# The last convolution's rows by way of scratch memory and a ring of four buffers

## The chip, the cores and the metric

One core of a Trainium2 chip runs the kernel. The metric is the time of one execution on the device, in microseconds (us), as the median of three runs. A profiled execution gives the trace from which all rows below are read.

## What is computed

The input x is 4 images of 64 channels and 128 x 128 pixels, float32. Four blocks follow one another, each with a residual and each on a group norm of what came before:

```python
x = x + L0(gn(x))   # super tokens and attention
x = x + L1(gn(x))   # grouped convolution, weights routed per image
x = x + L2(gn(x))   # depthwise convolutions, deformable sampling, selective scan
x = x + L3(gn(x))   # this change

def L3(x, w3, w1, b, p=4):
    m3 = (j - i) % p == 0                     # which input channels go through 3x3
    out = conv3x3(x, w3 * m3, padding=1)
    out = out + einsum('oi,bihw->bohw', w1 * ~m3, x)
    return out + b.sum(axis=1)
```

Only the last line of the four, the convolution L3 with its group norm, and the sampling and scan at the end of L2 concern this case.

## The kernel before

Images are worked in pairs: 2 images x 64 channels fill the 128 partitions, and `Fori(0, PAIRS)` runs the whole network twice, once per pair. Everything of a pair lies in `X` (128 x 128 rows x 128). Each engine has its own program written out in order; they meet through semaphores, and a wait on an engine holds all that stands behind it on that engine. All DMAs are issued by SP, on one queue.

The sampling and scan (`sample_and_scan_*`, lines 730 to 1005) walk over 32 chunks of four rows. DVE line 781 adds the block's result to a chunk of `X` and raises `sc_x`; the value `pair * NT + c + 1 + CREDIT` says that chunk c is final. The sampling reads its image from `PAD`, which shares its memory (`BIG`) with `RAW3`, so `RAW3` can be written only after the sampling.

The last convolution works with output rows in pairs and with one image at a time: `RAW3[half, q, j]` holds, for image q, the odd rows of X on partitions 0 to 63 and the even rows on 64 to 127, so that two output rows come from one matmul. `pair_rows(n)` (lines 501 to 512, SP) fills it in eight parts of 1 MB, two DMAs each (lines 508 and 511), from the moment at which all 32 chunks are final; part n waits until part n-2 has landed. Then SP waits for the last two parts (line 516) and begins its loop over the 16 strips of eight row pairs (NS = 16): wait for `cv_done` of strip S, two output DMAs (line 526), and, while another pair follows, the load of one strip of the next pair's input (line 456).

For a strip S the work goes: ACT `normed_rows(S)` (lines 1830 to 1844) norms its rows in place in `RAW3` and raises `l3_xn`; POOL (651, 652) and DVE (641, 642) make the four column sums; PE `columns_pe` (line 667, 16 matmuls) waits for `cv_done` of strip S-2, whose PSUM banks it takes; ACT `add_columns_act` (line 686) moves two of the four sums to `OBUF`, after the output DMA of strip S-2; DVE (692 to 697) adds the rest and raises `cv_done`. ACT's order is written out by hand:

```python
for S in range(3):
    normed_rows(S)
for S in range(NS):
    if S + 3 < NS:
        normed_rows(S + 3)
    add_columns_act(act, pair, S)
```

So on ACT the norm of strip S+3 stands ahead of the add of strip S.

Of the kernel before, what the change touches and what calls it, by code (L numbers as in the profile page):

```python
# [82 lines left out]
WTAIL = UNITS * UPIX - PROWS * PW  # L83
BACK = (UNITS // 2 + 2) * 16
PARTS3 = 8
SPREAD = [(WINDOWS + 1 - k) // 2 * 16 for k in range(2)]
MOVES = [n + PARTS3 * 16 for n in SPREAD]
EXPT = EXPERTS * 8 * 36
NRT = EXPT + FC + 2 * P

# [17 lines left out]
def program(nc, x, vec, mat, dts, rows, fc, sel, far_sel, cst, out):  # L108
    ctx = ExitStack()
    with ctx:  # L110
# [34 lines left out]
        IDB = sb("IDB", [P, P], BF16)  # L145
        RI = sb("RI", [P, 1], I32)
        spill, back_spill = (nc.dram_tensor(n, (WINDOWS, P, WROW * W), F32).ap() for n in ("spill", "back_spill"))
        rt_spill = nc.dram_tensor("rt_spill", (P, NRT), F32).ap()
        SMG = sb("SMG", [P, 160])
        UNIT, ROW16, CHAN8, HALF2, ROWPART = (sb(n, [P, w]) for n, w in  # L150
# [142 lines left out]
        r = Region()  # L293
        r.at = cols_end
        OBUF = r.take(2, 2 * CH)


        load = sem("load")
# [28 lines left out]
        l1_val, l1_tv, l1_tp, l1_mm, from_psum, l1_res, l1_st = steps(  # L327
            "l1_val", "l1_tv", "l1_tp", "l1_mm", "from_psum", "l1_res", "l1_st")
        moved, l1_back = [sem(f"moved{k}") for k in range(2)], sem("l1_back")
        l1_out = [sem(f"l1_out{k}") for k in range(RING)]  # L330
        cv_vector, cv_pool, cv_mm, cv_part, cv_done = (sem(n) for n in (
            "cv_vector", "cv_pool", "cv_mm", "cv_part", "cv_done"))
        rt_pe, rt_dve, rt_act = sem("rt_pe"), sem("rt_dve"), sem("rt_act")
# [67 lines left out]

        def parts_moved(pair, n):

            return pair * MOVES[n % 2] + SPREAD[n % 2] + (n // 2 + 1) * 32

        def strip_done(pair, c):

# [33 lines left out]
        @block.sync  # L441
        def _(sp):

            for lo in (0, C):
                sp.dma_start(VECS[lo:lo + C, :], vec).then_inc(load, 16)
                sp.dma_start(MATS[lo:lo + C, :], mat).then_inc(load, 16)
            sp.dma_start(DTS[:, :], dts).then_inc(load, 16)
            sp.dma_start(ROWV[:, :], rows).then_inc(load, 16)
            sp.dma_start(CSTS[:, :], cst).then_inc(load, 16)
            sp.dma_start(SELF, sel.rearrange("r t c -> r (t c)")).then_inc(load, 16)  # L450
            sp.dma_start(FSEL[:, :, :], far_sel).then_inc(load, 16)
            for k in range(2):
                sp.sem_inc(out_dma[k], 32)

            def load_strip(c, first_row):
                sp.dma_start(X[:, c * 8:c * 8 + 8, :], x[bass.ds(first_row, P), c * 8:c * 8 + 8, :]).then_inc(x_in[c // 4], 16)

            for c in range(NS):
                load_strip(c, 0)
            sp.wait_ge(const_act, 3)  # L460
            sp.dma_start(rt_spill, RT).then_inc(rt_saved, 16)
            with sp.Fori(0, PAIRS) as pair:

                def spread(w):

                    sp.wait_ge(moved[w % 2], pair * MOVES[w % 2] + (w // 2 + 1) * 16)
                    settle(sp)
                    sp.dma_start(WN[:, :, w * W:(w + 1) * W],
                                 spill[w].rearrange("(u c) (r x) -> (c r) u x", u=UNITS, x=W)).then_inc(l1_in, 16)

                for w in range(WINDOWS):
                    sp.wait_ge(o_x, pair * NS + (window_strip(w) + 1 + CREDIT))
                    if w == WINDOWS - 1:
                        sp.wait_ge(l1_sq, (pair + 1) * (2 * NS) + CREDIT)
                        for j in range(4):
                            sp.dma_start(FCT[:, 4 * j:4 * j + 4], fc[:, 4 * j:4 * j + 4]).then_inc(fc_in[j // 2], 16)
                    sp.dma_start(spill[w], X[:, STEP * w:STEP * w + WROW, :].rearrange("p r x -> p (r x)")).then_inc(moved[w % 2], 16)
                    if w >= 1:
                        spread(w - 1)
                spread(WINDOWS - 1)  # L480
                sp.dma_start(RT, rt_spill).then_inc(rt_in, 16)

                def back(u):

                    for v in (u, u + 1):
                        sp.wait_ge(l1_out[v % RING], pair * (UNITS // RING * 16) + (v // RING + 1) * 16)
                    sp.dma_start(X[u * WCH:(u + 2) * WCH, 1:H - 1, :].rearrange("c (v r) x -> c v (r x)", v=WINDOWS),
                                 back_spill[:, u * WCH:(u + 2) * WCH, W:(WROW - 1) * W].rearrange(
                                     "v c n -> c v n")).then_inc(l1_back, 16)

                for u in range(UNITS):
                    sp.wait_ge(l1_res, pair * UNITS + (u + 1))
                    sp.dma_start(back_spill[:, u * WCH:(u + 1) * WCH, :].rearrange("v c (r x) -> (c r) v x", x=W),
                                 OB1[:, u % RING, :].rearrange("p (v x) -> p v x", x=W)).then_inc(l1_out[u % RING], 16)
                    if u % 2 == 1 and u >= 3:
                        back(u - 3)
                back(UNITS - 2)
                for w, r, row in ((0, 0, 0), (WINDOWS - 1, WROW - 1, H - 1)):
                    sp.dma_start(X[:, row, :], back_spill[w, :, r * W:(r + 1) * W]).then_inc(l1_back, 16)

                def pair_rows(n):

                    if n >= 2:
                        sp.wait_ge(moved[n % 2], parts_moved(pair, n - 2))
                        settle(sp)
                    q, i = n // 4, n % 4
                    a = 16 * i + 1
                    sp.dma_start(RAW3[0:C, q, a:a + 16, 1:1 + W],
                                 X[q * C:(q + 1) * C, 2 * a - 1:2 * a + 30:2, :]).then_inc(moved[n % 2], 16)
                    lo, hi = (0 if i == 0 else a), min(a + 16, H // 2)  # L510
                    sp.dma_start(RAW3[C:P, q, lo:hi, 1:1 + W],
                                 X[q * C:(q + 1) * C, 2 * lo:2 * hi - 1:2, :]).then_inc(moved[n % 2], 16)

                sp.wait_ge(sc_x, (pair + 1) * NT + CREDIT)
                settle(sp)
                for n in range(PARTS3):
                    pair_rows(n)
                for n in (PARTS3 - 2, PARTS3 - 1):
                    sp.wait_ge(moved[n % 2], parts_moved(pair, n))
                    settle(sp)  # L520
                for S in range(NS):
                    q, t, k = S // 8, S % 8, S % 2
                    sp.wait_ge(cv_done, pair * NS + (S + 1 + CREDIT))
                    settle(sp)
                    for h in range(2):
                        sp.dma_start(out[bass.ds(pair * P + q * C, C), 16 * t + h:16 * t + 15 + h:2, :],
                                     OBUF[h * C:(h + 1) * C, k, :].rearrange("p (r w) -> p r w", r=8)).then_inc(out_dma[k], 16)
                    with sp.If(pair < PAIRS - 1):
                        load_strip(S, nc.s_assert_within(pair * P + P, 0, (PAIRS - 1) * P,
                                                         skip_runtime_bounds_check_because="the branch was taken"))  # L530
            for k in range(2):
                sp.wait_ge(out_dma[k], 32 * (PAIRS * NS // 2 + 1))
# [1023 lines left out]
        def _(pool):  # L1556
            credit(pool, cv_pool, df_w9, df_r1, df_lo, df_add, sc_u)
            pool.memset(PAD[:, :, :], 0.0).then_inc(border, 1)
            with pool.Fori(0, PAIRS) as pair:

                pool.wait_ge(border, pair * 3 + 1)
                pool.wait_ge(const_dve, 10)
                pool.wait_ge(rt_saved, 16)
                pool.wait_ge(cv_done, pair * NS + CREDIT)
                for k in range(2):
                    pool.wait_ge(out_dma[k], pair * (NS * 16) + 32)
# [50 lines left out]
        def _(act):  # L1617
# [18 lines left out]
                               banks(0, 3)[:, k * n:(k + 1) * n].rearrange("p (t k o) -> p k t o", t=9, k=8), ACT.Copy)  # L1636
            act.activation(FCB, PSUM[:, 3, 0:FC], ACT.Copy)
            act.activation(TO_CHANNEL, PSUM[:, 3, FC:FC + P], ACT.Copy).then_inc(const_act, 1)
            act.wait_ge(rt_saved, 16)
            settle(act)  # L1640

            def group_norm(n):
# [6 lines left out]
            with act.Fori(0, PAIRS) as pair:  # L1649
# [106 lines left out]
                def evacuate(u):  # L1756
# [2 lines left out]
                        act.wait_ge(l1_val, (pair + 1) * 16)  # L1759
                    if u >= RING:  # L1760
                        act.wait_ge(l1_st, pair * (2 * UNITS) + (2 * (u - RING) + 1))
                        act.wait_ge(l1_out[u % RING], pair * (UNITS // RING * 16) + (u // RING) * 16)
                    act.activation(OB1[:, u % RING, :].rearrange("p (a n) -> p a n", a=3),
                                   PSUM[:, 3 * (u % 2):3 * (u % 2) + 3, 0:3 * W], ACT.Identity,
                                   bias=SMW[:, 3, u:u + 1]).then_inc(from_psum, 1)
# [64 lines left out]
                def normed_rows(S):  # L1830

                    q, t = S // 8, S % 8
                    act.wait_ge(moved[S // 2 % 2], parts_moved(pair, S // 2))
                    settle(act)

                    def rows(lo, hi, j0, j1):
                        a = RAW3[lo:hi, q, j0:j1, 1:1 + W]
                        return act.activation(a, a, ACT.Identity, bias=NORM3[lo:hi, q, 0:1], scale=NORM3[lo:hi, q, 1:2])

                    if t == 0:  # L1840
                        rows(C, P, 0, 1)
                    if t == 7:
                        rows(0, C, ODD - 1, ODD)
                    rows(0, P, 8 * t + 1, min(8 * t + 9, ODD - 1)).then_inc(l3_xn, 1)
# [386 lines left out]
```

## Time and profile before

| | |
|---|---|
| median of three runs | 2919.49 us (2916.44 to 2926.07) |
| profiled execution, its own time | 2928.06 us |
| its span | 2926.2 us |
| PE busy | 2370.3 us, 81% of the span |
| DVE busy | 2004.0 us, 68% |
| ACT busy | 1412.5 us, 48% |
| POOL busy | 1119.8 us, 38% |
| DMA, mean over the span | 47 GB/s |
| BIG<-X, 512 KB each | 24 DMAs, median 8.6 us to landing |
| X<-x, 512 KB each | 32 DMAs, 7.5 us |
| out<-BIG, 256 KB each | 64 DMAs, 3.6 us |

The span holds two passes of the same work, one per pair; the last convolution of the first pair lies between about 1329 and 1477 us, that of the second between 2774 and 2926. A busy share over the whole span says little about a stage of 150 us; the rows for the change are those of these two stretches and of the sampling before them.

### The profile page before, as it was taken

To read this page: it belongs to the slowest core of one execution; us is meant where nothing else is said; L and a number is where in the kernel's file an instruction comes from. 1 tells how busy PE (TensorE), PEld (TensorE's weight loads), DVE (VectorE), ACT (ScalarE), POOL (GpSimd) and SP (SyncE) were. 2 spreads that over 40 slices of the span, in tenths; PEclk is the share of its full clock that TensorE was granted. 3 is DMA by queue.
4 is the path that set the end of the run, shared out by engine and by line. 5 is a ranking of instruction groups with operands and counts; after the bars stand their busy time and mean duration, and the time that the engine had idled before them with its cause. 6 is when DMAs were issued, how large, how long until landed. Compare 5 with 4: busy or idle time off the path is not lost.

```text
span 2926.2 us, 32644 instructions
## 1 busy us (share of the span) xinstructions
PE 2370.3 (81%) x8311; PEld 1249.8 (43%) x8311; DVE 2004.0 (68%) x3313; ACT 1412.5 (48%) x2140; POOL 1119.8 (38%) x967
## 2 busy tenths in 40 slices
PE   3897769599978888885968967786899688888778
PEld 2595535244433333332426954352344333333233
DVE  5544656398858999984555447464988589999844
ACT  2632433385754555552345336235677455555422
POOL 2200019280017777762311000374600377777422
PEclk9898889799979999997978989897999799999979
DMA  4000269500000000008610005492000000000083
GB/s 156 1 1 1 98 231 162 81 0 1 1 0 1 0 0 0 0 1 148 155 44 1 1 0 196 163 182 32 1 0 1 0 1 0 0 0 0 12 140 79
DMA packets 126795, 138.18 MB, mean 47 GB/s; under 512 B 3895, under 2 KB 106943, under 8 KB 123351
## 3 DMA queue, kind: packets, MB, share of 16 engines
q1 hardware_dynamic: 126679, 136.82, 20.3%
q8 instruction: 49, 0.80, 0.1%
q14 instruction: 67, 0.55, 0.1%
HBM read 64.65 MB, written 55.38 MB: 41 GB/s over the span
## 4 chain that ended last, share of the span: by engine, by line
PE 54%; DVE 18%; issue 10%; DMA 7%; ACT 5%; POOL 3%; DVEq 2%; SPq 1%; ACTq 0%; POOLq 0%
PE PSUM L1891 9%; PE PSUM L2069 7%; PE PSUM L667 6%; PE PSUM L959 4%; POOL BIG L868 3%; DMA BIG<-X 3%; DVE BIG L794 3%; PE PSUM L1934 2%; DVE BIG L770 2%; PE PSUM L2127 2%; PE PSUM L2121 2%; PE PSUM L2083 2%; PE PSUM L1948 2%; PE PSUM L953 2%; PE PSUM L1951 2%
## 5 line engine op out<-in xcount | busy, mean ns | idle before, releaser
L770 DVE TENSOR_TENSOR BIG<-PSUM,BIG 128x512 f32<-128x512 f32 x576 | 383.5, 684 | 100.7 <-POOL BIG L868 30.3
L1019 DVE SCALAR_TENSOR_TENSOR PSUM<-BIG,VECS,PSUM 128x1024 f32<-128x1024 f32 x272 | 350.3, 1288 | 119.7 <-PE PSUM L1891 113.4
L868 POOL TENSOR_TENSOR BIG<-BIG 128x512 f32<-128x512 f32 x256 | 346.0, 1351 | 147.5 <-DVE BIG L817 129.5
L708 POOL TENSOR_TENSOR BIG<-TOEP,BIG 128x384 f32<-128x384 f32 x84 | 97.1, 1182 | 611.6 <-DVE BIG L1417 611.6
L1891 PE MATMUL PSUM<-BIG,WDW 128*128 128x512 f32 x704 | 317.4, 601 | 9.0 <-ACT BIG L1802 9.0
L953 PE MATMUL PSUM<-BIG,SELB 120*128 120x512 bf16 x576 | 224.5, 392 | 120.1 <-DVE BIG L770 116.0
L959 PE MATMUL PSUM<-BIG,CSTS 128*128 128x512 f32 x512 | 270.5, 610 | 0.0
L849 POOL TENSOR_TENSOR BIG<-BIG 128x96 f32<-128x96 f32 x192 | 68.8, 384 | 382.3 <-ACT BIG L910 382.3
L1891 PEld LDWEIGHTS PSUM<-BIG,WDW 128*128 128x128 f32 x704 | 132.4, 191 | 168.4 <-issue 157.3
L953 PEld LDWEIGHTS PSUM<-BIG,SELB 120*128 120x128 bf16 x576 | 56.0, 97 | 345.7 <-DVE BIG L770 297.8
L2069 PE MATMUL PSUM<-BIG 128*128 128x381 f32 (+1 forms) x576 | 190.6, 495 | 15.2 <-DVE BIG L715 15.2
L667 PE MATMUL PSUM<-BIG,WL 128*128 128x512 f32 x256 | 126.0, 639 | 42.2 <-DVE BIG L697 26.0
L2069 PEld LDWEIGHTS PSUM<-BIG 128*128 128x128 f32 x576 | 112.0, 195 | 93.2 <-issue 20.6
L959 PEld LDWEIGHTS PSUM<-BIG,CSTS 128*128 128x128 f32 x512 | 101.8, 199 | 73.7 <-issue 63.9
L686 ACT ACTIVATE BIG<-PSUM,SM 128x512 f32<-128x512 f32 x64 | 42.5, 721 | 183.0 <-PE PSUM L667 140.6
L1595 POOL TENSOR_TENSOR BIG<-BIG 128x1024 f32<-128x1024 f32 x32 | 75.6, 2363 | 117.9 <-ACT BIG L1790 117.9
L692 DVE TENSOR_TENSOR BIG<-BIG,PSUM 128x512 f32<-128x512 f32 x32 | 22.4, 698 | 140.8 <-ACT BIG L686 140.8
L856 POOL TENSOR_TENSOR BIG<-BIG 128x320 f32<-128x320 f32 x64 | 98.8, 1544 | 42.7 <-ACT BIG L899 42.7
L667 PE MATMUL PSUM<-BIG,WMID 128*128 128x512 f32 x256 | 115.1, 592 | 0.0
L876 POOL TENSOR_TENSOR BIG<-BIG 128x512 f32<-128x512 f32 x64 | 108.7, 1699 | 13.5 <-DVE BIG L826 13.5
L651 POOL TENSOR_TENSOR BIG<-BIG 128x576 f32<-128x576 f32 x32 | 37.9, 1184 | 186.4 <-issue 110.3
L894 ACT ACTIVATE BIG<-PSUM 128x512 f32<-128x512 f32 x64 | 38.2, 597 | 145.6 <-DVE X L781 141.9
(347 smaller groups left out, 5276.9 us busy)
## 6 DMA issues: line engine op xcount, KB each, us to landing
spill<-X SPq DMA_DIRECT2D x18, 1024.0 KB, 6.4
back_spill<-BIG SPq DMA_DIRECT2D x32, 576.0 KB, 7.8
X<-x SPq DMA_DIRECT2D x32, 512.0 KB, 7.5
out<-BIG SPq DMA_DIRECT2D x64, 256.0 KB, 3.6
X<-back_spill SPq DMA_DIRECT2D x16, 1008.0 KB, 15.4
BIG<-X SPq DMA_DIRECT2D x24, 512.0 KB, 8.6
BIG<-fc SPq DMA_DIRECT2D x8, 1024.0 KB, 9.6
BIG<-X SPq DMA_DIRECT2D x4, 544.0 KB, 9.1
```

Source lines behind the costliest of these rows:

```text
L667: ins = pe.matmul(PSUM[:, 4 * k + m, :].rearrange("p (r j) -> p r j", r=8), w, VC[:, k, m, b:b + 8, :], start=(b == 0), stop=(b == 1))
L708: eng.tensor_tensor(to.rearrange("p (x c r) -> p x c r", x=3, r=WROW), TOEP[:, y].unsqueeze(1).unsqueeze(1).broadcast_to([P, 3, WCH, WROW] ...
L770: dve.tensor_tensor(img(o), img(PSUM[:, (k + q) % 2, :]), pch(c, XBASE, dy, dx), ALU.mult).then_inc(df_p, 1)
L794: dve.tensor_tensor_scan(HH[:, k, :], DA, UU, SM[:, 12:13] if first else HH[:, 1 - k, CH - 1:CH], ALU.mult, ALU.add).then_inc(sc_h, 1)
L856: pool.tensor_tensor(w9h, w9h, part(0), ALU.subtract).then_inc(df_r1, 1)
L868: pool.tensor_tensor(XS[:, k, :], XS[:, k, :], PRD[:, product_buffer(q), :], ALU.add).then_inc(df_add, 1)
L876: pool.tensor_tensor(UU, RL, XS[:, (k + 1) % 2, :], ALU.mult).then_inc(sc_u, 1)
L953: pe.matmul(PSUM[:, (k + q) % 2, :], SELB[:, q, :], WTB[0:WROWS, k, h * CH:(h + 1) * CH], start=True, stop=True).then_inc(df_w, 1)
L959: pe.matmul(PSUM[:, ACC, :], ident, PRD[:, m % 2, :], start=(m == 0), stop=(m == PE_SUMS - 1)).then_inc(df_acc, 1)
L1019: return dve.scalar_tensor_tensor(out=rows8(to), in0=strip(c, base, dy, dx), scalar=vc(weights, j), in1=rows8(acc), op0=ALU.mult, op1=ALU.add)
L1891: ins = pe.matmul(img(acc[:, h * CH:(h + 1) * CH]), w[:, j - stored, :], strip(c, base, dy, dx)[:, h * ROWS:(h + 1) * ROWS, :], start=(j = ...
L2069: ins = pe.matmul(to, WIDE[:, u % RING, x, :], v, start=(x == 1), stop=(x == 2))
```

## The change

The rows for the convolution no longer go from `X` to `RAW3` directly. `pair_rows(n)` now waits only until the chunks of its 16 rows of X are final, and writes them, split into odd and even rows, to a scratch tensor in device memory, `rows_spill`: four DMAs of 256 KB for each of the eight parts, the first seven of them while the sampling runs. A new `stage(S)` reads a strip's rows from there, 4 KB or 4.5 KB on each partition, into one of four buffers (`STAGE`), which lie in memory that the sampling used. Stages 0 to 3 are issued behind `pair_rows(7)`; stage S+4 is issued in SP's loop, after the wait for `cv_done` of strip S and the two output DMAs of S. `normed_rows(S)` waits for its stage instead of for the part, and writes from `STAGE` to `RAW3` instead of in place. The border rows of `rows_spill` are zeroed once at the start by four small DMAs, for which ACT and POOL wait together with the saving of the routing tables. The semaphores `l1_out` become `slot_dma` and count further, with no other effect on the block L1.

```diff
+STAGES = 4
-MOVES = [n + PARTS3 * 16 for n in SPREAD]
+MOVES = [n + PARTS3 * 32 for n in SPREAD]
...
+        rows_spill = nc.dram_tensor("rows_spill", (2, 2, C, ODD, W), F32).ap()
...
+        STAGE = r.take(STAGES, 9 * W)
...
             sp.dma_start(rt_spill, RT).then_inc(rt_saved, 16)
+            for q in range(2):
+                sp.dma_start(rows_spill[q, 0, :, 0, :], cs("zero")[0:C, 0:W]).then_inc(rt_saved, 16)
+                sp.dma_start(rows_spill[q, 1, :, ODD - 1, :], cs("zero")[C:P, 0:W]).then_inc(rt_saved, 16)
...
                 def pair_rows(n):
 
+                    sp.wait_ge(sc_x, pair * NT + (4 * n + 4 + CREDIT))
+                    settle(sp)
                     if n >= 2:
                         sp.wait_ge(moved[n % 2], parts_moved(pair, n - 2))
                         settle(sp)
-                    q, i = n // 4, n % 4
-                    a = 16 * i + 1
-                    sp.dma_start(RAW3[0:C, q, a:a + 16, 1:1 + W],
-                                 X[q * C:(q + 1) * C, 2 * a - 1:2 * a + 30:2, :]).then_inc(moved[n % 2], 16)
-                    lo, hi = (0 if i == 0 else a), min(a + 16, H // 2)
-                    sp.dma_start(RAW3[C:P, q, lo:hi, 1:1 + W],
-                                 X[q * C:(q + 1) * C, 2 * lo:2 * hi - 1:2, :]).then_inc(moved[n % 2], 16)
-
-                sp.wait_ge(sc_x, (pair + 1) * NT + CREDIT)
-                settle(sp)
+                    for q in range(2):
+                        sp.dma_start(rows_spill[q, 0, :, 8 * n + 1:8 * n + 9, :],
+                                     X[q * C:(q + 1) * C, 16 * n + 1:16 * n + 16:2, :]).then_inc(moved[n % 2], 16)
+                        sp.dma_start(rows_spill[q, 1, :, 8 * n:8 * n + 8, :],
+                                     X[q * C:(q + 1) * C, 16 * n:16 * n + 15:2, :]).then_inc(moved[n % 2], 16)
+
+                def stage(S):
+
+                    q, t = S // 8, S % 8
+                    if t == 0 or t == 6:
+                        for n in ((5, 6) if t == 0 else (7,)):
+                            sp.wait_ge(moved[n % 2], parts_moved(pair, n))
+                            settle(sp)
+                    if S >= STAGES:
+                        sp.wait_ge(l3_xn, pair * NS + (S - STAGES + 1))
+                        settle(sp)
+                    lo = 0 if t == 0 else 1
+                    sp.dma_start(STAGE[:, S % STAGES, lo * W:9 * W],
+                                 rows_spill[q, :, :, 8 * t + lo:8 * t + 9, :].rearrange("h c j x -> (h c) (j x)")).then_inc(
+                                     slot_dma[S % STAGES], 16)
+
                 for n in range(PARTS3):
                     pair_rows(n)
-                for n in (PARTS3 - 2, PARTS3 - 1):
-                    sp.wait_ge(moved[n % 2], parts_moved(pair, n))
-                    settle(sp)
+                for S in range(STAGES):
+                    stage(S)
                 for S in range(NS):
                     q, t, k = S // 8, S % 8, S % 2
                     sp.wait_ge(cv_done, pair * NS + (S + 1 + CREDIT))
@@
                         sp.dma_start(out[bass.ds(pair * P + q * C, C), 16 * t + h:16 * t + 15 + h:2, :],
                                      OBUF[h * C:(h + 1) * C, k, :].rearrange("p (r w) -> p r w", r=8)).then_inc(out_dma[k], 16)
+                    if S + STAGES < NS:
+                        stage(S + STAGES)
                     with sp.If(pair < PAIRS - 1):
...
-                pool.wait_ge(rt_saved, 16)
+                pool.wait_ge(rt_saved, 80)
...
-            act.wait_ge(rt_saved, 16)
+            act.wait_ge(rt_saved, 80)
...
                 def normed_rows(S):
 
                     q, t = S // 8, S % 8
-                    act.wait_ge(moved[S // 2 % 2], parts_moved(pair, S // 2))
+                    act.wait_ge(slot_dma[S % STAGES], pair * (UNITS // RING * 16 + NS // STAGES * 16)
+                                + (UNITS // RING * 16 + (S // STAGES + 1) * 16))
                     settle(act)
 
                     def rows(lo, hi, j0, j1):
-                        a = RAW3[lo:hi, q, j0:j1, 1:1 + W]
-                        return act.activation(a, a, ACT.Identity, bias=NORM3[lo:hi, q, 0:1], scale=NORM3[lo:hi, q, 1:2])
+                        a = STAGE[lo:hi, S % STAGES, (j0 - 8 * t) * W:(j1 - 8 * t) * W].rearrange("p (j x) -> p j x", x=W)
+                        return act.activation(RAW3[lo:hi, q, j0:j1, 1:1 + W], a, ACT.Identity,
+                                              bias=NORM3[lo:hi, q, 0:1], scale=NORM3[lo:hi, q, 1:2])
```

## Rows read from the trace of the kernel before

**Rows 1.** The page, part 4: the chain that ended last, by engine.

```profile
PE 54%; DVE 18%; issue 10%; DMA 7%; ACT 5%; POOL 3%; DVEq 2%; SPq 1%; ACTq 0%; POOLq 0%
```

**Rows 2.** Waits of SP's queue, 1320 to 1480: total us, times, longest us.

```profile
SPq L354 <- DVE X L781: 794.8, 1, 794.8
...
SPq L354 <- DMA BIG<-X: 19.5, 8, 5.8
```

**Rows 3.** Timeline of SP, first pair: start us, us, what it issues.

```profile
1329.48 0.69 SPq L508 DMA_DIRECT2D BIG<-X  x1
...
1406.79 1.40 SPq L526 DMA_DIRECT2D out<-BIG  x2
1408.33 0.80 SPq L456 DMA_DIRECT2D X<-x  x1
...
1475.41 1.41 SPq L526 DMA_DIRECT2D out<-BIG  x2
```

**Rows 4.** Timeline of ACT, both pairs' last convolutions.

```profile
1337.89 2.88 ACT L1838 ACTIVATE BIG<-BIG,SM 64x128 f32<-64x128 f32 x3 [3.75 <-DMA BIG<-X]
...
1402.70 1.34 ACT L686 ACTIVATE BIG<-PSUM,SM 128x512 f32<-128x512 f32 x2 [3.71 <-PE PSUM L667]
...
2828.72 1.24 ACT L1838 ACTIVATE BIG<-BIG,SM 128x1024 f32<-128x1024 f32 x1
2829.94 1.33 ACT L686 ACTIVATE BIG<-PSUM,SM 128x512 f32<-128x512 f32 x2
```

**Rows 5.** Timeline of PE, both pairs' last convolutions; [idle before <-releaser].

```profile
1343.20 6.75 PE L667 MATMUL PSUM<-BIG,WL 128*128 128x512 f32 x8 [8.09 <-POOL BIG L652]
...
1386.81 5.45 PE L667 MATMUL PSUM<-BIG,WL 128*128 128x512 f32 x8 [12.83 <-DVE BIG L697]
...
1395.53 3.60 PE L667 MATMUL PSUM<-BIG,WL 128*128 128x512 f32 x8
...
1402.39 3.60 PE L667 MATMUL PSUM<-BIG,WL 128*128 128x512 f32 x8
...
2787.87 6.34 PE L667 MATMUL PSUM<-BIG,WL 128*128 128x512 f32 x8 [8.13 <-POOL BIG L652]
...
2797.47 3.60 PE L667 MATMUL PSUM<-BIG,WL 128*128 128x512 f32 x8
```

**Rows 6.** Windows: length, busy per engine, PEclk, DMA share, GB/s; sampling, PE's first strip.

```profile
880.00:1325.00 445.00, 373.08 (x1139) 154.17 (x1137) 391.87 (x559) 239.49 (x455) 326.58 (x302) 0.98 0.00 0
...
1343.00:1350.00 7.00, 6.80 (x9) 0.54 1.25 185
```

**Rows 7.** Landings, issue to landing: lines 456, 526 (1370 to 1490), 508, 511.

```profile
DMA to landing us min/median/max: 4.7/5.2/6.0
DMA to landing us min/median/max: 3.2/3.6/5.0
DMA to landing us min/median/max: 5.0/8.4/9.7
DMA to landing us min/median/max: 7.6/10.6/10.9
```

**Rows 8.** Timeline of DVE, both pairs' last convolutions.

```profile
1356.76 0.69 DVE L697 TENSOR_TENSOR BIG<-BIG,PSUM 128x512 f32<-128x512 f32 x1
...
1404.08 0.70 DVE L692 TENSOR_TENSOR BIG<-BIG,PSUM 128x512 f32<-128x512 f32 x1 [3.01 <-ACT BIG L686]
...
2801.01 0.68 DVE L697 TENSOR_TENSOR BIG<-BIG,PSUM 128x512 f32<-128x512 f32 x1
...
2920.42 0.68 DVE L697 TENSOR_TENSOR BIG<-BIG,PSUM 128x512 f32<-128x512 f32 x1
```

**Rows 9.** Timeline of PE in the block before, four matmuls after a gap.

```profile
834.37 3.47 PE L2121 MATMUL PSUM<-BIG,CSTS 128*128 128x512 f32 x4 [4.04 <-DVE BIG L1019]
```

**Rows 10.** Timeline of ACT at the start of the kernel.

```profile
53.61 1.28 ACT L1650 ACT_TABLE_LOAD   x1 [3.64 <-DMA rt_spill<-BIG]
56.85 0.26 ACT L1644 ACTIVATE SM<-PSUM,GNE 128x1 f32<-128x1 f32 x1 [1.97 <-PE PSUM L1885]
```

More of the change, by code:

```diff
@@ L329, in program @@
         moved, l1_back = [sem(f"moved{k}") for k in range(2)], sem("l1_back")
-        l1_out = [sem(f"l1_out{k}") for k in range(RING)]
+        slot_dma = [sem(f"slot_dma{k}") for k in range(RING)]
         cv_vector, cv_pool, cv_mm, cv_part, cv_done = (sem(n) for n in (
@@ L402, in parts_moved @@
         def parts_moved(pair, n):
-            return pair * MOVES[n % 2] + SPREAD[n % 2] + (n // 2 + 1) * 32
+            return pair * MOVES[n % 2] + SPREAD[n % 2] + (n // 2 + 1) * 64
         def strip_done(pair, c):
@@ L485, in back @@
                     for v in (u, u + 1):
-                        sp.wait_ge(l1_out[v % RING], pair * (UNITS // RING * 16) + (v // RING + 1) * 16)
+                        sp.wait_ge(slot_dma[v % RING], pair * (UNITS // RING * 16 + NS // STAGES * 16) + (v // RING + 1) * 16)
                     sp.dma_start(X[u * WCH:(u + 2) * WCH, 1:H - 1, :].rearrange("c (v r) x -> c v (r x)", v=WINDOWS),
@@ L493, in _ @@
                     sp.dma_start(back_spill[:, u * WCH:(u + 1) * WCH, :].rearrange("v c (r x) -> (c r) v x", x=W),
-                                 OB1[:, u % RING, :].rearrange("p (v x) -> p v x", x=W)).then_inc(l1_out[u % RING], 16)
+                                 OB1[:, u % RING, :].rearrange("p (v x) -> p v x", x=W)).then_inc(slot_dma[u % RING], 16)
                     if u % 2 == 1 and u >= 3:
@@ L1761, in evacuate @@
                         act.wait_ge(l1_st, pair * (2 * UNITS) + (2 * (u - RING) + 1))
-                        act.wait_ge(l1_out[u % RING], pair * (UNITS // RING * 16) + (u // RING) * 16)
+                        act.wait_ge(slot_dma[u % RING], pair * (UNITS // RING * 16 + NS // STAGES * 16) + (u // RING) * 16)
                     act.activation(OB1[:, u % RING, :].rearrange("p (a n) -> p a n", a=3),
```

## The prediction

> **What bounds the kernel now.** The page comes first: the chain of work that ended last is PE for 54%, with DMA at 7% [rows 1]. That is the whole span; the change lives in two stretches of some 150 us and in the samplings before them, so the waits and timelines of those stretches decide. The waits of SP's queue [rows 2] show SP idle for 794.8 us until the last chunk of X is final (DVE line 781) and then held 19.5 us in eight waits by its own moves to RAW3. SP's timeline shows the first move at 1329.48 [rows 3]; ACT gets its first rows at 1337.89, 8.4 us later [rows 4]; PE's first strip starts at 1343.20 after 8.09 us idle, and PE stops once more for 12.83 us before 1386.81 [rows 5]. That second gap has a DVE releaser, but ACT's queue explains it: its add of strip 2 could not write OBUF before the output of strip 0, which SP issues only after all its moves. So the moves cost the head of the stretch and one gap in its middle. From 1395.53 on PE takes a strip of 16 matmuls every 6.86 us (1395.53 to 1402.39) with no gap: there PE is the bound, and DMA, ACT, DVE and POOL keep up.
>
> **The change, part by part.** *Removed*: the seven first parts leave the end of the sampling, and SP's wait for parts 6 and 7 ahead of its strip loop. The 12.83 us gap goes with it.
>
> *Moved into the sampling*: 28 DMAs of 256 KB per pair. In 445 us of sampling the DMA share is 0.00, and SP has nothing else to issue [rows 6, 2]. What it could cost is DVE's reading of X beside them. I take 0; if each DVE instruction became 1% longer it would be 4 us a pair (391.87 us busy), and below zero nothing can come, as no engine gives work away. The end of the sampling stays.
>
> *Head*: behind the last chunk now come part 7 (four DMAs, the same 1 MB as part 0 had) and stage 0 behind it in the same queue. Part 0 landed 8.4 us after its issue; stage 0 adds 4.5 KB x 128 partitions. In pairs of moves the first lands after 8.4 us and the second, issued about 0.7 us later, after 10.6 [rows 7]: 2.9 us apart for half a megabyte each, so one follows the other instead of sharing. An input strip of about that size, issued 1.54 us behind an output of 512 KB, lands in 5.2, so one of these larger pieces takes about 2 us itself. I take 2.15 us later for ACT's first norm and PE's start; bounds 0 (shared engines, both done with part 7) and 4. Stages 1 to 3 follow at about 2 us each, by 1347, before PE ends strip 0 at about 1355: nothing waits for them.
>
> *The ring, which is where the time goes.* Stage S+4 is issued after `cv_done` of S. On ACT its norm, `normed_rows(S+4)`, stands ahead of `add_columns_act(S+1)`. What waits behind ACT's new wait is therefore that add, and with it DVE's adds and `cv_done` of S+1, which releases stage S+5. Four buffers do not open this circle: the wait binds ACT's order, not the data that PE reads next. One turn, from SP's output issue of one strip to that of the next:
> - output issues until the next DMA: 1406.79 to 1408.33 [rows 3], 1.54;
> - landing. The nearest row is the input strip X<-x, which stands in exactly this place behind the same output, comes from device memory, has 512 KB and 4 KB per partition: 5.2 (4.7 to 6.0) [rows 7];
> - ACT wakes: 0.05;
> - the norm until the add behind it starts: 2828.72 to 2829.94 [rows 4], 1.22;
> - add until DVE's first add: 1402.70 to 1404.08 [rows 4, 8], 1.38;
> - DVE's four adds until SP's next issue: 1404.08 to 1406.79 [rows 8, 3], 2.71.
>
> The sum is 12.10 us against PE's 6.86. Stages 4 to 15 each make one turn: 12 turns, 145.2 us per pair. In the second pair no input strip is issued behind the stage; by the order seen above that changes nothing.
>
> *Tail*: after `cv_done` of strip 12 only PE binds. Strip 14 starts about 0.1 us ahead of that strip's output issue, two strips take 13.7, and from the end of PE's strip to SP's issue it is 4.4 (1402.39 to 1406.79) [rows 5, 3]: 18.0. PE now has gaps of about 5 us between strips. After a gap of 4.04 us four matmuls took 3.47 [rows 9], as slow as the first eight of a strip after 8.09 (6.75), in whose window the granted clock was 0.54, so mostly 1.2 GHz [rows 6]; eight at 2.4 GHz take 3.43 (half of the 6.86). Such a strip takes 10.2 us instead of 6.9. That still fits into a turn of 12.1; in the tail it can cost 0 to 3.3, and I take 1.6.
>
> *Start*: four small DMAs behind rt_spill. ACT waited for rt_spill until 53.6, loaded a table for 1.28 and then waited 1.97 us more for PE [rows 10]; that wait covers them. 0, at most 1. The two other new waits on SP (parts 5 to 7, `l3_xn`) are for things long done; what is queued behind them is only the strip loop. The norm keeps its size.
>
> **The sum.** First pair: the first output can be issued at 1357.45 (end of line 697 of strip 0) + 0.22, that is 1357.67 [rows 8]. Then 1357.67 + 2.15 + 145.2 + 18.0 + 1.6 = 1524.6 for the issue of the last output, which was 1475.41 [rows 3]: +49.2. Second pair: 2801.69 + 0.22 + 167.0 = 2968.9, against 2921.1 + 0.22 = 2921.3 [rows 8]: +47.5. Together +96.7 us. The profiled execution took 2928.06, so its like becomes 3024.8. The median of the runs lies 8.6 us below it, and 2919.49 + 96.7 = **3016.2 us**, 3.3% slower.
>
> The Trainium skill ("DMA: Bandwidth & Descriptors", section "Anatomy of one DMA — SWDGE (gpsimd) path") gives a DMA about 2.0 us fixed plus its bytes at 436 GB/s, measured on another issuing path than SP's; for a stage an estimate from it is 3.2 us, and 2968 in all. The traced 5.2 us contradicts it for a transfer behind another, and the sum goes by the trace.
>
> **Rivals.**
> - *Short landing* (0.05): the stage lands as fast as a lone output does, 3.2 us [rows 7], if the output ahead does not delay it. Each of the 24 turns is 2.0 shorter: 2968. Against it: X<-x in the same place never took under 4.7. This is the time that the page's fit gives.
> - *PE takes the turn* (0.05): if PE's clock stayed at 1.2 GHz for all matmuls a strip would take 13.7, more than 12.1, and bind: 24 x 1.6 = +38, 3055. Against: a PE without gaps has been at 2.4 GHz after its first eight matmuls each time.
> - *The landing is later* (0.07): in the first pair the next input strip, issued 0.8 us behind the stage, shares the engines with it. With 8.4 us, as a BIG<-X that had another behind it, 12 turns grow by 3.2: +38, 3055. The 2.9 us distance speaks against.
> - *Faster, because the ring hides the fetch* (0.02): place, ACT's wait for the stage. If that wait never ended last, PE would run on from 1345.35: first strip 10.0, fifteen by 6.86, 4.4, so the last issue at 1462.7 (-12.8); in the second pair from 2790.0 with 9.6 for the first strip [rows 5], 2906.9 (-14.4): 2892. It decides against the forecast only if a turn is under 8.1 us (12.1 - 96.7 / 24), which needs a landing in 1.2. No landing in [rows 7] is near. It could only be right if I read ACT's order wrongly.
> - *The writes do not go beside the sampling* (0.01): if they slowed it or came at its end as before, the gain at the head goes too; seven parts per pair at 5.8 us (twice the 2.9) are +81, 3097.
>
> **How the numbers follow.** The forecast has 0.80. Its own bounds: landings of 4.7 to 6.0 give -12 to +19 over 24 turns, the head -4 to +4, the tail -3 to +3, start and sampling 0 to +9: 2997 to 3051. To leave out no more than 0.2 in all, and as the two rivals at 3055 lie just beyond, the range is 2995 to 3056. A measurement of this kernel can tell about 0.3% (9 us) from no change; every case but the fourth is slower by more: slower 0.97, same 0.01, faster 0.02.
>
> **What the profile after would show.** SP issues at line 526 some 12 us apart for strips 1 to 12 and 7 apart at the end. ACT's norm released by DMA BIG<-rows_spill twelve times per pair, 4 to 6 us each, and its add directly behind the norm. PE idle about 2 or 5 us before each strip. The gap of 12.83 gone, PE's start in the stretch some 2 us later. DMA in the sampling above zero, with DVE's busy time there unchanged. The prediction is wrong if the outputs stay 6.9 us apart, or if the landing of a stage is not near 5.2.

## The result, and the profile after

The changed kernel takes 3022.55 us (median of four runs, 3020.13 to 3023.89) against 2922.78 for the kernel before, run beside it. The ratio is 1.0347, with a 95% interval from 1.0333 to 1.0361: 3.5% slower, about 100 us, where 96.7 and 3016.2 us had been forecast. The profiled executions took 2928.06 and 3023.75 us.

Line numbers of the new kernel are some 20 higher: ACT's norm is line 1859 (was 1838), its add 706 (686), DVE's adds 712 to 717 (692 to 697), PE's matmuls 687 (667), the stage 531, the outputs 544 (526).

The page, parts 1, 4 and 6. DVE, ACT and POOL are busy for the same time as before; PE is busy 30 us longer with the same matmuls, because more of them ran at a lower granted clock (see "PE's clock" below). In the chain DMA has risen from 7% to 8%, and a line that did not exist before stands third in it:

```profile
PE 2400.3 (79%) x8311; PEld 1257.1 (42%) x8311; DVE 2004.2 (66%) x3313; ACT 1412.2 (47%) x2140; POOL 1121.4 (37%) x967
...
PE 48%; DVE 19%; issue 11%; DMA 8%; ACT 6%; POOL 3%; DVEq 2%; SPq 2%; ACTq 0%; POOLq 0%
PE PSUM L1913 9%; PE PSUM L2091 6%; DMA BIG<-rows_spill 4%; PE PSUM L979 4%; POOL BIG L888 3%; DVE BIG L814 3%; PE PSUM L1956 2%; PE PSUM L687 2%; DVE BIG L790 2%; PE PSUM L2149 2%; PE PSUM L1970 2%; PE PSUM L2105 2%; PE PSUM L2143 2%; PE PSUM L973 2%; PE PSUM L2131 2%
...
BIG<-rows_spill SPq DMA_DIRECT2D x28, 512.0 KB, 5.4
```

The same line in part 5 says who waits for it: ACT's norm. In the kernel before it also waited for DMAs, but 13.2 us in all and only at the head of the stretches [rows 4]; now it waits 246.6 us in all:

```profile
L1859 ACT ACTIVATE BIG<-BIG,SM 128x1024 f32<-128x1024 f32 (+2 forms) x40 | 42.7, 1080 | 246.7 <-DMA BIG<-rows_spill 246.6
```

The timeline of SP in the first pair's last convolution, to set beside [rows 3]. The outputs, 6.8 us apart before, are 11.9 to 13.0 apart here for strips 0 to 12; the DMA of a stage is mostly issued 1.5 to 1.7 us behind the first output DMA:

```profile
1329.17 0.57 SPq L515 DMA_DIRECT2D rows_spill<-X  x1
...
1358.11 1.49 SPq L544 DMA_DIRECT2D out<-BIG  x2
...
1395.51 1.42 SPq L544 DMA_DIRECT2D out<-BIG  x2
1397.05 0.81 SPq L531 DMA_DIRECT2D BIG<-rows_spill  x1
...
1408.02 1.42 SPq L544 DMA_DIRECT2D out<-BIG  x2
...
1507.44 1.41 SPq L544 DMA_DIRECT2D out<-BIG  x2
...
1528.07 1.40 SPq L544 DMA_DIRECT2D out<-BIG  x2
```

One turn of the circle, as the chain of work that ended last shows it, each step released by the one above it: the DMA, then the two pieces of a norm, the add, DVE's adds, the outputs, the next DMA. No PE instruction is in it:

```profile
1397.05 5.41 DMA BIG<-rows_spill
1402.50 0.07 issue
1402.57 0.09 ACT BIG L1859
...
1402.97 1.12 ACT BIG L1859
1404.09 1.20 ACT BIG L706 x2
1405.31 0.06 DVE BIG L712
...
1407.11 0.69 DVE BIG L717
...
1408.02 0.62 SPq L544
...
1409.69 5.50 DMA BIG<-rows_spill
```

Twice in the first pair (at 1420.81 and 1481.89) the view goes over a strip of PE's instead of a DMA. The add that follows there belongs to the strip before that one, whose matmuls had ended 11.6 and 14.1 us earlier; PE's end and the norm's end only fall together in time. In the second pair no such step stands between the DMAs.

ACT and PE in the same stretch, beside [rows 4] and [rows 5]. ACT waits 10 us for a stage, norms it, and only then, with no idle time between, adds a strip whose matmuls were long done (PE had ended strip 2 at 1367.5, and its add starts at 1379.12). PE's releaser is DVE's last add: PE waits for PSUM banks that are still held until the late adds of an earlier strip are done.

```profile
1377.97 1.24 ACT L1859 ACTIVATE BIG<-BIG,SM 128x1024 f32<-128x1024 f32 x1 [10.13 <-DMA BIG<-rows_spill]
1379.12 1.29 ACT L706 ACTIVATE BIG<-PSUM,SM 128x512 f32<-128x512 f32 x2
1390.33 1.24 ACT L1859 ACTIVATE BIG<-BIG,SM 128x1024 f32<-128x1024 f32 x1 [9.92 <-DMA BIG<-rows_spill]
```

```profile
1344.66 5.69 PE L687 MATMUL PSUM<-BIG,WL 128*128 128x512 f32 x8 [9.99 <-POOL BIG L672]
...
1370.41 3.70 PE L687 MATMUL PSUM<-BIG,WL 128*128 128x512 f32 x8 [2.89 <-DVE BIG L717]
1373.94 3.60 PE L687 MATMUL PSUM<-BIG,WMID 128*128 128x512 f32 x8
1382.98 5.33 PE L687 MATMUL PSUM<-BIG,WL 128*128 128x512 f32 x8 [5.44 <-DVE BIG L717]
```

The sampling, the window of [rows 6]: DVE's busy time is 391.64 us against 391.87, with a DMA share of 0.07 where it was 0.00.

```profile
880.00:1325.00 445.00, 371.77 (x1139) 153.69 (x1137) 391.64 (x559) 239.97 (x456) 326.81 (x302) 0.98 0.07 17
```

### The profile page after: what moved, and what is told of

Its sections match the earlier page's. It is cut to its first block, busy times and chain, and to the rows that moved or that the text cites. A ratio compares the mean times of both kernels' runs of the same rounds, so it can differ in the third digit from the quotient of the medians.

```text
span 3021.9 us, 32766 instructions
## 1 busy us (share of the span) xinstructions
PE 2400.3 (79%) x8311; PEld 1257.1 (42%) x8311; DVE 2004.2 (66%) x3313; ACT 1412.2 (47%) x2140; POOL 1121.4 (37%) x967
## 4 chain that ended last, share of the span: by engine, by line
PE 48%; DVE 19%; issue 11%; DMA 8%; ACT 6%; POOL 3%; DVEq 2%; SPq 2%; ACTq 0%; POOLq 0%
PE PSUM L1913 9%; PE PSUM L2091 6%; DMA BIG<-rows_spill 4%; PE PSUM L979 4%; POOL BIG L888 3%; DVE BIG L814 3%; PE PSUM L1956 2%; PE PSUM L687 2%; DVE BIG L790 2%; PE PSUM L2149 2%; PE PSUM L1970 2%; PE PSUM L2105 2%; PE PSUM L2143 2%; PE PSUM L973 2%; PE PSUM L2131 2%
## 5 line engine op out<-in xcount | busy, mean ns | idle before, releaser
L687 PE MATMUL PSUM<-BIG,WL 128*128 128x512 f32 x256 | 158.5, 777 | 105.1 <-DVE BIG L717 85.4
L2091 PE MATMUL PSUM<-BIG 128*128 128x381 f32 (+1 forms) x576 | 189.0, 492 | 15.2 <-DVE BIG L735 15.2
L1859 ACT ACTIVATE BIG<-BIG,SM 128x1024 f32<-128x1024 f32 (+2 forms) x40 | 42.7, 1080 | 246.7 <-DMA BIG<-rows_spill 246.6
L687 PEld LDWEIGHTS PSUM<-BIG,WL 128*128 128x128 f32 x256 | 61.8, 251 | 198.2 <-DVE BIG L717 105.2
L896 POOL TENSOR_TENSOR BIG<-BIG 128x512 f32<-128x512 f32 x64 | 108.8, 1700 | 13.5 <-DVE BIG L846 13.5
```

The lines of the kernel that those rows point to most:

```text
L687: ins = pe.matmul(PSUM[:, 4 * k + m, :].rearrange("p (r j) -> p r j", r=8), w, VC[:, k, m, b:b + 8, :], start=(b == 0), stop=(b == 1))
L896: pool.tensor_tensor(UU, RL, XS[:, (k + 1) % 2, :], ALU.mult).then_inc(sc_u, 1)
L2091: ins = pe.matmul(to, WIDE[:, u % RING, x, :], v, start=(x == 1), stop=(x == 2))
```

## The experiments

The theory: SP issues stage S+4 behind the outputs of strip S, and its norm stands on ACT ahead of the add of strip S+1, so that each output waits for a whole fetch that began behind the output before. This closed chain is called the circle, and one round of it a turn. The rivals: the queue or the ring cannot deliver strips fast enough whatever the order; PE at its lower clock sets the turn; the writes slow the sampling.

**Norm two strips ahead instead of three** (e1), one number on ACT, four buffers and all DMAs as in the change:

```diff
-                for S in range(3):
+                for S in range(2):
                     normed_rows(S)
                 for S in range(NS):
-                    if S + 3 < NS:
-                        normed_rows(S + 3)
+                    if S + 2 < NS:
+                        normed_rows(S + 2)
```

> Change kept, but ACT norms two strips ahead of its adds instead of three. Theory (the circle): the norm of strip S+4 now stands ahead of the add of S+2, so the way from one output issue over stage, landing, norm and add spans two strips, 12.4 us for two, 6.2 each, under PE's 6.87; PE binds again and the outputs come 6.87 us apart. From PE's start 15.4 us behind the last chunk: 15.4 + 9.1 + 15 x 6.87 + 4.4 = 131.9 us per pair against 145.9 and 147.2 before: 2893 us, 1% faster than the kernel before. Rival (four buffers or the DMA queue cannot feed the strips, whatever ACT's order): stays near 3022, outputs 12.4 apart. Rival (PE's low clock sets the turn): no change either, since the PE program is the same.

Measured: 2895.04 us, ratio to before 0.991 (0.9893 to 0.9927). ACT's timeline of this kernel shows why. The norm still waits for its stage, but 3 us instead of 10, and the add behind it then waits for PE again, which the right-hand column names:

```profile
1363.37 1.35 ACT L706 ACTIVATE BIG<-PSUM,SM 128x512 f32<-128x512 f32 x2 [4.36 <-PE PSUM L687]
1367.70 1.24 ACT L1859 ACTIVATE BIG<-BIG,SM 128x1024 f32<-128x1024 f32 x1 [2.98 <-DMA BIG<-rows_spill]
1370.29 1.33 ACT L706 ACTIVATE BIG<-PSUM,SM 128x512 f32<-128x512 f32 x2 [1.34 <-PE PSUM L687]
1374.49 1.26 ACT L1859 ACTIVATE BIG<-BIG,SM 128x1024 f32<-128x1024 f32 x1 [2.87 <-DMA BIG<-rows_spill]
1377.11 1.34 ACT L706 ACTIVATE BIG<-PSUM,SM 128x512 f32<-128x512 f32 x2 [1.35 <-PE PSUM L687]
```

The adds are 6.9 and 6.8 us apart, and PE has no idle time in the stretch behind its start. Norming less far ahead took 127 us off the change, with the same four buffers, the same bytes and the same queue. That rules out that the ring, the queue or the bandwidth set the turn of 12.3 us.

**Stage released earlier** (e2): the same circle opened at its other end, on SP.

```diff
                 for S in range(NS):
+                    if S + STAGES < NS:
+                        stage(S + STAGES)
                     q, t, k = S // 8, S % 8, S % 2
                     sp.wait_ge(cv_done, pair * NS + (S + 1 + CREDIT))
...
-                    if S + STAGES < NS:
-                        stage(S + STAGES)
```

> Change kept, but SP issues stage S+4 ahead of its wait for cv_done of S (it still waits for the norm of S, whose buffer it takes). Theory (the circle): the stage is then released one strip earlier, the way spans two strips less the output issues, (12.4 - 1.6) / 2 = 5.4 us a strip, PE binds with 6.87: 2893 us. Rival (landing or bandwidth too slow for the strips): near 3022.

Measured: 2892.94 us, ratio 0.9902 (0.9885 to 0.9918), as expected; the outputs are 6.86 us apart in the mean ((1461.21 - 1358.36) / 15). Either end of the circle opens it.

**Stage ahead of the outputs** (e3): the circle stays closed, its longest term is shortened.

```diff
                     sp.wait_ge(cv_done, pair * NS + (S + 1 + CREDIT))
                     settle(sp)
+                    if S + STAGES < NS:
+                        stage(S + STAGES)
                     for h in range(2):
...
-                    if S + STAGES < NS:
-                        stage(S + STAGES)
```

> Change kept, but stage S+4 is issued between the wait for cv_done of S and the two output DMAs instead of behind them. The circle stays over one strip. Theory (a landing is long because the output stands ahead in the queue): the 1.6 us of output issues leave the turn and the landing falls from 5.4 to between 3.2 and 4.0: turn about 9.0 to 9.4, 24 turns 3.1 shorter, about 2950 (2940 to 2960). Rival (a stage takes 5.4 to land wherever it stands): only the 1.6 goes, turn 10.7, 2984.

Measured: 2945.49 us, ratio to before 1.0087 (1.007 to 1.0104), inside the 2940 to 2960 of the theory. SP's timeline of this kernel, and the landings of all its stages:

```profile
1376.74 0.33 SPq L531 DMA_DIRECT2D BIG<-rows_spill  x1
1377.27 1.41 SPq L546 DMA_DIRECT2D out<-BIG  x2
1378.83 1.27 SPq L459 DMA_DIRECT2D X<-x  x1
1385.67 0.33 SPq L531 DMA_DIRECT2D BIG<-rows_spill  x1
```

```profile
DMA to landing us min/median/max: 3.5/3.7/7.3
```

A stage without outputs ahead lands in 3.7 us, not 5.4, and the turn is 9.0 in the first pair (outputs of strips 0 and 12 at 1359.36 and 1467.31). The turn became 3.3 us shorter, and 24 times that is 79 us; the kernel became 77 us faster.

**Input strip ahead of the stage** (e4), which acts in the first pair alone:

```diff
-                    if S + STAGES < NS:
-                        stage(S + STAGES)
                     with sp.If(pair < PAIRS - 1):
                         load_strip(S, ...)
+                    if S + STAGES < NS:
+                        stage(S + STAGES)
```

> Change kept, but in the loop the next pair's input strip is issued ahead of the stage instead of behind it; this acts in the first pair alone. Theory (circle, DMAs of the queue follow one another): each of the first pair's 12 turns grows by the issue, 0.9 us, and by the 2 us that half a megabyte takes, 2.9 in all, from 12.44 to 15.3, and the second pair keeps 12.17: 3022 + 35 = 3057. Rival (transfers share the engines, the order does not matter): only 0.9 more, 3033. Rival (stage not on the path): no change.

Measured: 3037.48 us (two runs, 3035.00 and 3039.95), 15 more than the change. That lies between the theory's 3057 and the 3033 of the rival by which the order of the transfers does not matter, and much nearer to the rival. The first pair's turn grew from 12.44 to 13.90, the second pair's stayed (12.13), so the stage is on the path. But half a megabyte issued ahead of it cost 1.5 us and not 2.9: the issue took its 0.9, and the landing grew only from 5.5 to 6.0. Beyond the time of the issue the order of these two transfers cost little:

```profile
DMA to landing us min/median/max: 5.5/6.0/6.6
```

**Stages 0 to 3 ahead of part 7** (e5), on top of e2:

```diff
-                for n in range(PARTS3):
+                for n in range(PARTS3 - 1):
                     pair_rows(n)
+                sp.wait_ge(sc_x, (pair + 1) * NT + CREDIT)
+                settle(sp)
                 for S in range(STAGES):
                     stage(S)
+                pair_rows(PARTS3 - 1)
...
```

> As e2 (stage S+4 ahead of the wait for cv_done of S), and stages 0 to 3 issued ahead of part 7, from the moment at which all chunks are final; they need only parts 0 to 4, which landed long ago. Theory (stage 0 landed late because 1 MB of part 7 stands ahead of it): it lands 3.7 us after its issue as a stage without an output ahead did, ACT's first norm starts when the group norm's values are there, 5.9 us behind the last chunk instead of 10.1, and PE's start and the end of each pair come about 4 us earlier: 2893 - 8 = 2885 us, 1.2% faster than the kernel before. Rival (the head is set by the group norm chain or by POOL's sums): 2893, as e2.

Measured: 2885.49 us, ratio to before 0.988 (0.9865 to 0.9895), the fastest of all and within 1 us of the theory's 2885; the kernel before is 35 us slower. ACT's first norm is no longer released by a DMA but by the values of the group norm:

```profile
1334.32 5.14 ACT L1862 ACTIVATE BIG<-BIG,SM 64x128 f32<-64x128 f32 x5 [1.79 <-DVE SM L1555]
```

It starts 6.2 us behind SP's first issue at 1328.16, where it was 10.2 in the change (1329.17 to 1339.33).

**Writes beside the sampling, alone** (e6): the kernel before, with parts 0 to 6 written to scratch memory as the change writes them; nobody reads them.

```diff
...
+                for n in range(PARTS3 - 1):
+                    sp.wait_ge(sc_x, pair * NT + (4 * n + 4 + CREDIT))
+                    settle(sp)
+                    for q in range(2):
+                        sp.dma_start(rows_spill[q, 0, :, 8 * n + 1:8 * n + 9, :],
+                                     X[q * C:(q + 1) * C, 16 * n + 1:16 * n + 16:2, :]).then_inc(load, 16)
+                        sp.dma_start(rows_spill[q, 1, :, 8 * n:8 * n + 8, :],
+                                     X[q * C:(q + 1) * C, 16 * n:16 * n + 15:2, :]).then_inc(load, 16)
+                sp.wait_ge(load, pair * ((PARTS3 - 1) * 64) + (16 * 9 + (PARTS3 - 1) * 64))
+                settle(sp)
                 sp.wait_ge(sc_x, (pair + 1) * NT + CREDIT)
```

> The kernel before, with the change's writes of parts 0 to 6 to scratch memory during the sampling (28 DMAs of 256 KB per pair), whose data nobody reads; the moves from X to RAW3 stay as before. This measures what the writes cost the sampling. Theory: 0, so 2920 us, ratio 0.999 to 1.001, DVE's busy time in the sampling unchanged. Rival (reading X beside DVE slows it by 1% or more): +8 us or more, 2928.

Measured: 2920.74 us beside 2920.59, ratio 1.0 (0.9991 to 1.001). The writes cost nothing that could be told from zero, at most 0.1% or 3 us in both pairs together.

**What sets the turn: three kernels.** e7 has two buffers and norms one strip ahead; e8 has four and norms one ahead; e10 has four, norms two ahead and releases stage S+3. First e7; the counts of `slot_dma` that go with two buffers are left out of its diff:

```diff
-STAGES = 4
+STAGES = 2
...
-                for S in range(3):
+                for S in range(1):
                     normed_rows(S)
                 for S in range(NS):
-                    if S + 3 < NS:
-                        normed_rows(S + 3)
+                    if S + 1 < NS:
+                        normed_rows(S + 1)
```

> Change kept with two buffers instead of four, and ACT norming one strip ahead instead of three, so that the difference of the two (one strip) stays. Stage S+2 is issued after cv_done of S and its norm stands ahead of the add of S+1. Theory (the turn is set by buffers minus strips normed ahead, not by the number of buffers): outputs 12.2 to 12.5 apart as with four buffers, 3022 to 3030 us. Rival (depth of the ring sets the pace): half the buffers make it clearly slower, 3100 or more.

Measured: 3084.35 us, 54 above the theory's range and 16 under the rival's 3100: it bears out neither. Two things were left out of the expectation. Stages 2 to 15 make 14 turns per pair, not 12; and a turn took 13.5 us (outputs of strips 0 and 14 at 1359.44 and 1548.94; 13.2 in the second pair). The timeline of DVE in this kernel shows the difference:

```profile
1380.92 0.76 DVE L665 TENSOR_TENSOR BIG<-BIG 128x576 f32<-128x576 f32 x1 [8.43 <-ACT BIG L1863]
1381.60 1.71 DVE L666 TENSOR_TENSOR BIG<-BIG 128x576 f32<-128x576 f32 x1
1383.23 0.68 DVE L716 TENSOR_TENSOR BIG<-BIG,PSUM 128x512 f32<-128x512 f32 x1
```

With one strip ahead DVE's column sums need the norm just done, and they stand ahead of its adds: they start at 1380.92, and the adds at 1383.23 instead of about 1382.10 (1.31 behind ACT's add at 1380.79, as in the change). That is 1.1 us a turn, about what the first pair's turn has grown by. e8 asks whether norming one strip ahead costs something by itself, with the circle open:

```diff
-                for S in range(3):
+                for S in range(1):
                     normed_rows(S)
                 for S in range(NS):
-                    if S + 3 < NS:
-                        normed_rows(S + 3)
+                    if S + 1 < NS:
+                        normed_rows(S + 1)
```

> Change kept with its four buffers, ACT norming one strip ahead. The norm of S+4 stands ahead of the add of S+3, so the way from output to output spans three strips. This asks what made the kernel with two buffers and one strip ahead slow. Theory (the number of strips between a stage's release and the add behind its norm sets the turn): PE binds, outputs 6.87 apart, 2893 us. Rival (one strip ahead is too little for the column sums and PE in any case): slower than 2893 by the wait of PE for POOL in each strip, 2 us a strip or 64 in all, 2957.

Measured: 2893.18 us, outputs 6.86 apart. With the circle open, one strip ahead costs nothing. It cannot tell why e7 was slow, because e7's circle was closed. e10 closes the circle again by other numbers, with four buffers and without DVE waiting for the norm just done:

```diff
-                for S in range(STAGES):
+                for S in range(3):
                     stage(S)
...
-                    if S + STAGES < NS:
-                        stage(S + STAGES)
+                    if S + 3 < NS:
+                        stage(S + 3)
...
-                for S in range(3):
+                for S in range(2):
                     normed_rows(S)
                 for S in range(NS):
-                    if S + 3 < NS:
-                        normed_rows(S + 3)
+                    if S + 2 < NS:
+                        normed_rows(S + 2)
```

> Change with its four buffers, but stage S+3 (not S+4) issued after cv_done of S, and ACT norming two strips ahead (not three). The difference between the strip that is released and the strip normed ahead stays one, the numbers themselves both change. Stages 3 to 15 make 13 turns instead of 12. Theory (the turn is set by that difference alone, as long as DVE's column sums do not need the norm just done, as they did with one strip ahead): turns of 12.2 to 12.5 as in the change, one more per pair in the place of a strip of 6.9: 3022 + 2 x 5.5 = 3033. Rival (the lead over the output sets the pace, fewer strips in flight are slower): 12.8 a turn or more, 3046 or more.

Measured: 3028.48 us (3033 expected, the rival 3046 or more), with turns of 12.47 us in the first pair (13 from 1352.91 to 1515.08) and 12.16 in the second (2851.55 to 3009.64), against 12.44 and 12.17 in the change. So the turn follows the difference between the strip that an output releases and the strip that ACT norms ahead of its add: one strip gives 12.3 us, two (e1, e2) or three (e8) give PE's pace. e7 agrees only once its 1.1 us on DVE is allowed for, which is read from its timeline and was not tried by itself. A ring of three buffers has no measurement: in e10 three stages are in flight, but the ring has four.

## Why the prediction was right, point by point

**The circle** was read from ACT's order alone and came out as said: 24 turns, each term in its place, and the chain of the trace goes the same way. The forecast turn was 12.10; measured are 12.44 in the first pair ((1507.44 - 1358.11) / 12) and 12.17 in the second ((2999.05 - 2852.97) / 12). The second pair's is within 0.1 of the sum. In the first pair the landing is the larger term: 5.5 us in the median where 5.2 had been taken from the input strips [rows 7]. Three of the twelve stages also feed a norm with a small border piece, which the sum left out. That adds 0.3 to 0.5 to their turns. The rest of the difference between the pairs is mostly landing: the ring's stages landed in 5.5 us in the first pair and 5.3 in the second, in e10 5.5 and 5.2, in e8 5.7 and 5.3. The forecast had said that the input strip behind the stage, which only the first pair has, changes nothing. It is the likely cause of these 0.2 to 0.4 us, but it was not tried by itself. If it is the cause, the rival of the later landing had the sign right and the size, 3.2 us, far too large.

**The sum.** The stretch is measured from SP's first issue behind the last chunk to its last output issue. The first pair took 198.9 us (1329.17 to 1528.07) where the forecast gave 195.1 (1329.48 to 1524.6). The second took 193.0 (2824.09 to 3017.04; the last start is worked out, as the rows there group four strips' outputs) where it gave 194.8. The head came 1.4 and 1.1 us earlier than forecast, the turns 4.1 and 0.9 later, the tail 1.0 later and 1.6 earlier (20.6 and 18.0 where 18.0 + 1.6 had been taken). Together that is 2 us more; 2.7 less between the two stretches and 0.3 less ahead of the first make 95.6 of 96.7, and the profiled executions differ by 95.7 (the medians by 99.8). The turns, 145 us of each pair's 195, were earned. That the whole agrees to 1 us is luck: misses of 1 to 4 us in head, turns and tail have either sign.

**The head.** PE starts 15.5 and 15.2 us behind SP's first issue, 1.8 and 1.4 later than before; forecast were 2.15. In the first pair the first output came only 0.8 us later than before, as PE's first eight matmuls took 5.69 us where they had taken 6.75 [rows 5]; the forecast had not reckoned with that. That stage 0 stands behind part 7 in the queue is the cause of the late start: with it ahead (e5) the first norm came 4 us earlier.

**The landing.** The forecast took the landing of a transfer behind two outputs, and its size was right. e3 shows that the place behind them is what makes it long: 3.7 us without the outputs ahead, 5.4 with them. The size given to half a megabyte in 4 KB pieces, 2 us, was too much: in e5 four stages issued 0.43 us apart landed 4.1 to 7.1 us after their issues. If the first took 4.1 and the last 7.1, they landed (3 x 0.43 + 7.1 - 4.1) / 3 = 1.4 us apart, an estimate. The estimate from the page "DMA: Bandwidth & Descriptors" of the Trainium skill (section "Anatomy of one DMA — SWDGE (gpsimd) path"), 3.2 us for a stage, is close to the 3.7 of a stage that has the queue to itself and 2.2 short of one behind an output. The rival of the short landing was wrong for this kernel; a landing near its 3.2 us is seen only with the stage issued ahead of the outputs.

**The sampling** cost 0, as taken (e6). **The start** cost 0: ACT's wait for PE behind its table load fell from 1.97 to 0.54 us and so still covers the four small DMAs.

```profile
55.05 1.28 ACT L1670 ACT_TABLE_LOAD   x1 [5.07 <-DMA rows_spill<-CSTS]
56.87 0.26 ACT L1664 ACTIVATE SM<-PSUM,GNE 128x1 f32<-128x1 f32 x1 [0.54 <-PE PSUM L1907]
```

**PE's clock** was lower behind most gaps, as foreseen: in the first pair the first eight matmuls took 5.18 to 6.62 us in ten of the twelve strips 3 to 14, and the granted clock was 0.68 in such a group (1382.98 to 1388.10) and 1.00 in the eight matmuls behind it. It did not set the turn: PE waited 2.2 to 5.4 us for DVE before each of these strips all the same, and was busy for 101 of these 145 us:

```profile
1365.00:1510.00 145.00, 101.03 (x186) 40.94 (x185) 47.50 (x75) 31.44 (x41) 27.23 (x24) 0.86 0.45 123
```

**ACT's wait** for a stage was forecast at 4 to 6 us and is 9.3 to 10.2. The forecast's own terms leave about 9.6 of its turn of 12.1 once the norm (1.22) and the add (1.3) are taken off, so this sign of the profile did not fit its own sum. The sum itself does not use it.

**The rival on the other side** named its own condition, a fetch hidden behind the ring, and priced it at 2892 us. e1, e2 and e8 fulfil that condition and measure 2895, 2893 and 2893. So the idea of the change is sound and worth 1%; what was wrong with it is one number, how far ACT norms ahead.

## What to carry to other kernels

The slack of a ring is not its number of buffers: count how many strips lie between the event that releases a fetch and the first instruction, in the consumer's own queue, that stands behind the wait for it and leads back to that event. If that is one strip, a whole fetch is paid per strip; it was so with four buffers (the change, e10) and with two (e7). If it is more, the way from output to output is shared among that many strips: 12.4 us over two strips is 6.2 each, less than PE's 6.86, and PE binds again (e1). Release a buffer by the instruction that empties it and not by the end of the strip's whole work (e2), and issue a fetch that something waits for ahead of the stores that nobody waits for (e3).

## What the runs showed of the hardware

- Issuing a stage takes 0.33 us when nothing was issued just before it (e3) and 0.8 behind two output DMAs of 256 KB.
- A transfer landed 1.5 us later with half a megabyte in pieces of 4 KB issued ahead of it, the 0.9 us of that issue included (e4), and four such transfers landed about 1.4 us apart (e5, the estimate above). For half a megabyte in pieces of 512 bytes, from SBUF to SBUF, the like estimate is 2.9 us: 0.7 + 10.6 - 8.4 [rows 7].
- In the first pair PE's first eight matmuls of a strip took 3.7 us after gaps of 2.89 and 3.12 us, and 5.2 to 6.6 after ten gaps from 2.20 to 5.44; the granted clock was 0.70 in the first group below and 1.00 in the second. Gaps of about 3 us were seen with either outcome.

```profile
1420.81 5.18 PE L687 MATMUL PSUM<-BIG,WL 128*128 128x512 f32 x8 [2.99 <-DVE BIG L717]
...
1469.43 3.70 PE L687 MATMUL PSUM<-BIG,WL 128*128 128x512 f32 x8 [3.12 <-DVE BIG L717]
```
